# Weighted sums stored as they are and gathered by transfers, own lists at the layers' ends, all chunks between the layers normalised on ScalarE

## The chip, the core and the metric

One of the eight cores of a Trainium2 chip runs the whole program. The metric is the time of one execution in microseconds (us) on the device. The engines are TensorE (PE; its weight loads stand as PEld in the profile), VectorE (DVE), ScalarE (ACT), GpSimd (POOL) and SyncE (SP), whose queue issues all the transfers of this kernel.

## What is computed

Two transformer layers on the same activations, batch 4, sequence 1024, width 128, 16 heads of 8, all in float32. Layer 1's attention is causal; its weights are scaled up, so exact maxima matter. Both layers share the FFN weights (integers with a scale).

```python
x = x + attn_a(layernorm(x))     # qkv = x @ Wqkv + b, heads of (q 8, k 8, v 8)
x = x + ffn(layernorm(x))        # (silu(x Wg^T) * (x Wu^T)) Wd^T, hidden 384
x = x + attn_b(layernorm(x))     # as attn_a, keys after the query masked out
x = x + ffn(layernorm(x))
# attention: softmax(q k^T / sqrt(8)) v, heads side by side, @ Wout + bout
```

## The kernel before

The activations x stay in SBUF, in 8 chunks of 512 rows (4 tiles of 128). For the attention, q and k are split in two parts (for exact products in a faster format), stored to DRAM and loaded again head by head. A **window** is one batch element and a group of four heads: 16 windows per layer, of 1024 queries by 1024 keys each. A window has two **halves** f of 512 queries.

For each window there are these kinds of work, and a hand-written string of letters (`order` of a `Plan`) sets their order on every engine. The same walk over the string is run by all five engines, and each takes from it what is its own.

- `j`, a job: TensorE multiplies 128 queries by up to 512 keys (line 1146) into one bank of a ring of four (layer 1: three), and VectorE reduces it to row maxima (lines 923, masked 919, paired 900). The next job in that bank waits for it (`ring_free`). Jobs run ahead of the window to which they belong, 48 in layer 0 and 37 in layer 1.
- `h`, `H`: the negated maxima of half 0 (of the next window) or half 1, split in two bfloat16 parts by GpSimd (lines 559, 561), are turned on TensorE (line 1198), copied by ScalarE (line 696) and put by SP as two rows into the query operand (line 439), so that the score product subtracts them itself. After `H`, SP also loads the operands of the window two further on: 14 transfers.
- `s`, scores: keys by 512 queries (line 1180, causal mask 1188) for one head (layer 1: two heads), and ScalarE's exponential of it (line 680). A unit takes a bank, or a pair of banks, of the ring of units. In the last window of layer 0, from step `wide_step` = 5 on, units have two heads each (wide) in a ring of two bank pairs.
- `p`, sums: four heads' probabilities by v and a column of ones (line 1214) into bank 7. So bank 7 holds, for each head, 8 rows of sums and one of denominators, over 512 queries. After the last step of a half ScalarE copies the bank to `sums` (line 687), and the next half's sums wait for that.
- `N`, `n`: the sums of half 0 or 1 are turned: four 128x128 transposes on TensorE (line 1072), ScalarE copies the useful columns to `att_raw` (line 701), VectorE inverts the denominators (line 954), GpSimd multiplies (line 569) into `att`, rows by queries. They also take a place in the ring of units.

A window of layer 0 has 64 jobs, 64 units and 16 sums, one of layer 1 has 36, 24 and 12.

After the attention come output projection and FFN, chunk by chunk, in `turn(m, projected, ffn_rows, ffn, residual, turned, qkv_rows)`, each argument the chunk on which that step works in turn m. For chunk m+3 ScalarE gathers the heads of four windows (`gather_heads`, line 710), TensorE turns them (`transpose_ot`), ScalarE copies them (`copy_ot`, line 717). For chunk m+2: projection (line 1230), addition to x (line 831), moments (812, 816), GpSimd's inverse deviation (530, 532), normalisation (823). Chunk m+1: turn, gate and up products (1285), SiLU (781), product (1001). Chunk m: down product (1301), addition, and in layer 0 moments again and the normalisation for layer 1, on VectorE (`normalise`, line 823) for chunks 0 to 5 and on ScalarE (`normalise_tail`, line 773) for chunks 6 and 7. Chunk m-1 (layer 0): q, k, v of layer 1 (lines 1083, 1085), their split (652, 851) and store. Chunks 0 and 1 begin already in the last window (`early_chunk`, `project_at`). The first 18 to 22 jobs of layer 1 stand in the last turns of layer 0.

## Time and profile before

| | us |
|---|---|
| median of 3 runs (lowest, highest) | 1311.12 (1311.08, 1314.08) |
| the profiled execution, as timed | 1309.93 |
| its span from first to last instruction | 1308.1 |
| steady windows of layer 0, each | 39.46 |
| steady windows of layer 1, each | 25.92 |

| from, to (us) | what runs |
|---|---|
| 0 to 66 | layer 0's q, k, v, first jobs |
| 66 to 659 | windows 0 to 14 of layer 0 |
| 659 to 704 | window 15 of layer 0, with the beginnings of chunks 0 and 1 |
| 704 to 814 | projection, FFN, q, k, v of layer 1, its first jobs |
| 814 to 1215 | windows 0 to 14 of layer 1 |
| 1215 to 1242 | window 15 of layer 1 |
| 1242 to 1308 | projection and FFN of layer 1, stores |

How to read it: the page gives busy time per engine over the whole span, which mixes stages with different limits. So the stretches (busy time of each engine between two times) and the chain of waits within a stretch are of more use. Neighbouring instructions of an engine overlap, so the busy time of a group is less than count times mean, and the distance between two starts is what one costs in a row. An instruction that doesn't wait for a semaphore may still be held because its engine works in order.

### The profile page before, as it was taken

The page shows a single profiled execution, that of the slowest core. Times are in us where ns is not written, and L with a number is a line of the kernel's source. Part 1 is how long each engine was busy: PE and PEld are TensorE (multiplying, and loading weights), DVE is VectorE, ACT ScalarE, POOL GpSimd, SP SyncE. Part 2 cuts the span into 40 slices and gives each one's busy share as a digit, 9 for nine tenths or more (in the row PEclk, how much of TensorE's full clock was granted, in tenths as well). Part 3 has the DMA queues.
Part 4 walks back from the last instruction along what each step waited for, and adds up shares of the span by engine and source line. Part 5 has one row for each costly group of instructions (what it writes and reads, how often), then busy time and mean ns, then how long its engine had stood idle before and what let it go on. Part 6 is the DMA issues. An engine that isn't in the chain of part 4 may idle for free.

```text
span 1308.1 us, 26669 instructions
## 1 busy us (share of the span) xinstructions
PE 1266.3 (97%) x9681; PEld 646.3 (49%) x9681; DVE 1158.3 (89%) x2969; ACT 1005.4 (77%) x1799; POOL 148.4 (11%) x315
## 2 busy tenths in 40 slices
PE   8899999999999999999997998999999999999898
PEld 6434343434344434334334775555555555555487
DVE  8699999999999999999943888899999999999276
ACT  8678888888888888888885554677777777787743
POOL 5630000000000000000001222200000000000111
PEclk9689999999999999999998998799999999999999
DMA  7611011111011111011000263113111211220001
GB/s 217 204 33 34 16 20 34 34 35 34 9 27 34 34 34 33 6 31 35 1 3 1 65 161 97 35 37 63 37 36 41 59 37 35 45 57 3 2 26 41
DMA packets 40059, 58.43 MB, mean 45 GB/s; under 512 B 7796, under 2 KB 19448, under 8 KB 39928
## 3 DMA queue, kind: packets, MB, share of 16 engines
q1 hardware_dynamic: 39928, 56.72, 18.5%
q8 instruction: 77, 1.26, 0.4%
q14 instruction: 54, 0.44, 0.1%
HBM read 36.77 MB, written 18.87 MB: 43 GB/s over the span
## 4 chain that ended last, share of the span: by engine, by line
PE 88%; DVE 5%; ACT 3%; issue 2%; DMA 0%; POOL 0%; SPq 0%; DVEq 0%; ACTq 0%; POOLq 0%
PE psum L1214 30%; PE psum L1146 22%; PE psum L1180 20%; PE psum L1072 3%; PE psum L1301 3%; PE psum L1285 2%; PE psum L1188 2%; ACT probs L680 2%; DVE maxima L923 1%; PE psum L1083 1%; PE psum L1230 1%; DVE hid L1001 1%; PE psum L1121 1%; PE psum L1198 1%; PE psum L1057 1%
## 5 line engine op out<-in xcount | busy, mean ns | idle before, releaser
L680 ACT ACTIVATE probs<-psum 128x512 f32<-128x512 f32 (+3 forms) x1386 | 822.1, 669 | 166.1 <-PE psum L1180 87.4
L923 DVE TENSOR_REDUCE maxima<-psum 128x1 f32<-128x512 f32 x1232 | 768.4, 681 | 25.2 <-PE psum L1146 22.6
L1180 PE MATMUL psum<-qop,kop 64*128 64x512 f32 (+3 forms) x1792 | 512.7, 421 | 9.1 <-ACT probs L680 7.5
L1146 PE MATMUL psum<-kop,qop 62*128 62x512 f32 (+2 forms) x1744 | 497.9, 424 | 2.0 <-DVE maxima L919 1.0
L1214 PE MATMUL psum<-probs,v 128*32 128x512 f32 (+3 forms) x3584 | 435.4, 561 | 0.8 <-ACT sums L687 0.8
L1180 PEld LDWEIGHTS psum<-qop,kop 64*128 64x128 f32 x1792 | 254.7, 187 | 212.8 <-ACT probs L680 187.4
L1146 PEld LDWEIGHTS psum<-kop,qop 62*128 62x128 f32 x1744 | 251.2, 187 | 206.5 <-DVE maxima L923 90.7
L919 DVE CUSTOM_DVE_ANT_0 junk<-psum,mask 128x384 bf16<-128x384 f32 (+3 forms) x512 | 222.5, 485 | 14.6 <-PE psum L1146 14.0
L1214 PEld LDWEIGHTS psum<-probs,v 128*32 128x32 f32 x3584 | 72.1, 108 | 112.5 <-issue 84.5
L1188 PE MATMUL psum<-half_ident,key_mask 64*128 64x64 bf16 x1024 | 83.0, 196 | 0.0
L559 POOL TENSOR_TENSOR shift<-negmax,zeros 128x16 bf16<-128x16 f32 x64 | 14.2, 222 | 546.2 <-DVE negmax L931 546.2
L569 POOL TENSOR_TENSOR att<-att_raw,rden 128x128 f32<-128x128 f32 x64 | 26.1, 408 | 421.6 <-DVE rden L954 421.6
L1285 PE MATMUL psum<-ffn_xt,gate_up_w 128*128 128x512 f32 x192 | 53.4, 414 | 6.1 <-DVE hid L1001 6.0
L831 DVE TENSOR_TENSOR x<-psum,x 128x512 f32<-128x512 f32 x32 | 22.1, 690 | 40.2 <-PE psum L1230 26.8
L1188 PEld LDWEIGHTS psum<-half_ident,key_mask 64*128 64x128 bf16 x1024 | 45.6, 96 | 19.2 <-issue 7.9
L1301 PE MATMUL psum<-down_w,hid 128*128 128x128 f32 x384 | 47.6, 280 | 4.7 <-DVE hid L1001 4.7
L781 ACT ACTIVATE hid<-psum 128x512 f32<-128x512 f32 x48 | 28.5, 598 | 30.5 <-PE psum L1285 30.2
L1301 PEld LDWEIGHTS psum<-down_w,hid 128*128 128x128 f32 x384 | 45.0, 194 | 7.6 <-DVE hid L1001 7.2
L647 ACT ACTIVATE qk<-psum,bqk 128x512 f32<-128x512 f32 x32 | 21.2, 683 | 31.2 <-PE psum L1083 31.1
L919 DVE DVE_READ_ACCUMULATOR2_ANT maxima<- 128x1 f32 x512 | 42.5, 83 | 0.0
L1285 PEld LDWEIGHTS psum<-ffn_xt,gate_up_w 128*128 128x128 f32 x192 | 34.2, 191 | 14.8 <-DVE hid L1001 8.5
L1072 PE MATMUL psum<-ident,sums 128*128 128x128 f32 x256 | 38.7, 283 | 2.3 <-ACT sums L687 1.6
(106 smaller groups left out, 735.6 us busy)
## 6 DMA issues: line engine op xcount, KB each, us to landing
qop<-q_parts SPq DMA_DIRECT2D x256, 64.0 KB
kop<-k_parts SPq DMA_DIRECT2D x64, 128.0 KB
kop<-k_parts SPq DMA_DIRECT2D x128, 64.0 KB
q_parts<-parts SPq DMA_DIRECT2D x24, 256.0 KB, 2.9
k_parts<-parts SPq DMA_DIRECT2D x24, 256.0 KB, 3.2
x<-in_L_attn_a_x SPq DMA_DIRECT2D x8, 256.0 KB, 4.3
q_parts<-att SPq DMA_DIRECT2D x8, 256.0 KB, 3.7
k_parts<-att SPq DMA_DIRECT2D x8, 256.0 KB, 3.8
```

Of the source, the lines that this page charges most:

```text
L569: nc.gpsimd.tensor_tensor(dst, att_raw[:, f, :, :, 0:HD], rden[:, f].rearrange("p t (h o) -> p t h o", o=1).broadcast_to([P, TPC, HG, HD]) ...
L680: nc.scalar.activation(probs[:, slot, heads[0] % 2:heads[-1] % 2 + 1, c0:], psum[:, bank:bank + len(heads), c0:], ACT.Exp, scale=SCORE_SCA ...
L781: nc.scalar.activation(hid[:, c, :], psum[:, 2 + 2 * (c % 2), :], ACT.Silu, scale=DEQUANT).then_inc(silu_ready, 1)
L919: ins = nc.vector.tensor_tensor_reduce(out=junk[:, slot, column:column + width], in0=src, in1=mask[:, CHUNK - width:], scale=1.0, scalar=L ...
L923: ins = nc.vector.tensor_reduce(dst, src, AX_X, ALU.max)
L1072: ins = nc.tensor.transpose(psum[:, bank, t * P:(t + 1) * P], src[:, t, :], ident[:])
L1146: ins = mm(psum[:, bank, column:column + width], qop[rows, buf, f, r, qb * P:(qb + 1) * P].bitcast(F32R), kop[rows, buf, r, kh * CHUNK:kh ...
L1180: ins = mm(psum[:, bank + k, c0:], kop[rows, buf, c // 2, j * P:(j + 1) * P].bitcast(F32R), qop[rows, buf, f, c // 2, c0:].bitcast(F32R), ...
L1188: ins = mm(psum[:, bank + k, at:at + TILE_ROWS], key_mask[rows, part, :], half_ident[rows], start=False, stop=part == 1)
L1214: ins = mm(psum[32 * c:32 * c + 32, 7, c0:], v[:, at:at + 32], probs[:, slot, c % 2, c0:], start=(j == 0), stop=(s == plan.half_end[f]), t ...
L1285: ins = mm(psum[:, 2 + 2 * (c % 2) + k, :], gate_up_w[:, k, c, :].bitcast(F32R), ffn_xt[:, part].bitcast(F32R), start=part == 0, stop=part ...
L1301: ins = mm(psum[:, 7, t * P:(t + 1) * P], hid[:, c, t * P:(t + 1) * P], down_w[:, c, :], start=(c == 0), stop=(c == FB - 1))
```

## The change

1. The turns of the sums (`N`, `n`), their copy, the reciprocals of a half, GpSimd's products per half, the gather of the heads and the turn of a chunk with its copy are gone. Instead SP stores each `sums` tile to DRAM (`head_sums`). Per batch element it loads the denominators (as 128 rows of 64) and the heads' rows straight into `att`, which now has the width on the partitions and queries along them, as the projection wants its operand. VectorE inverts the denominators once, SP stores them and loads them broadcast over the 8 rows of a head, and GpSimd multiplies. For batch elements 0 to 2 this happens in windows 5 to 7, 9 to 11 and 13 to 15, for the last one in the turns: load after the last sums, reciprocal at the end of turn 0, product in turn 2.
2. A `Plan` has three strings, `opening`, `order` and `closing`, in place of one with offsets. In the steady windows the order of jobs, scores, sums and shifts is as it was, without `N` and `n`. The opening of layer 0 is the old one. In the opening of layer 1, 32 jobs stand before the first scores instead of 38, and 74 before window 1, as before. The closings are new: in layer 0 wide units (`S`) begin with step 4 and have a ring of three bank pairs; chunk 0 is projected at step 11 and turned for the FFN at step 14, in bank 6. In layer 1 the sums of window 14 come before the last shift.
3. `ASIDE_CHUNK` = 0: for all chunks ScalarE does the normalisation between the layers, after the second SiLU and before the third, and GpSimd the two small steps for its bias.
4. After the last window TensorE waits for the copy of the last sums, where it waited for the copy of the turned ones.

```diff
+WIDE_RING = 3
 TAIL_CHUNK = CHUNKS - 2
+ASIDE_CHUNK = 0
...
+        for letter in opening + order * (WINDOWS - 2) + closing:
+            if letter == "j":
...
+            elif letter in "sS":
+                w, x = units_begun // len(units), units[units_begun % len(units)]
+                if letter == "S":
+                    x = x[0], (x[1][0], x[1][0] + 1)
+                    self.wide_from = min(self.wide_from, taken)
+                assert letter == "S" or taken < self.wide_from
+                units_begun += 1 + (letter == "S")
...
+            return (unit - self.wide_from) % WIDE_RING * 2
+            return unit - min(unit - self.wide_from, WIDE_RING - 1)
...
 PLANS = [Plan(causal=False, heads=HEAD_UNITS, unit_ring=3, job_ring=4, alternate=True,
-              order="sjjsjpsjjjsspsjjsjspsjjsjspsjsjsjjsjssjjsjspHssjjsjpsjjsjspjjsjsspjsjssjsjjsnjsjjsspjssjsjpjssjsjpjssjsjpsjjsjspsjjsjspsjjsjsjsjsjsNhjjsjsspssjjjsps",
-              jobs_ahead=48, sums_behind=2, project_at=(9, 11, 14), wide_step=5),
+              opening="jjjjjjjjjjjjjjjjjjjjjjjjjjjjjjjjjjjjjjjjjjhjjjjjjsjjsjsjjjsssjjsjspsjjsjspsjsjsjjsjssjjsjspHssjjsjpsjjsjspjjsjsspjsjssjsjjsjsjjsspjssjsjpjssjsjpjssjsjpsjjsjspsjjsjspsjjsjsjsjsjshjjsjsspssjjjsps",
+              order="sjjsjpsjjjsspsjjsjspsjjsjspsjsjsjjsjssjjsjspHssjjsjpsjjsjspjjsjsspjsjssjsjjsjsjjsspjssjsjpjssjsjpjssjsjpsjjsjspsjjsjspsjjsjsjsjsjshjjsjsspssjjjsps",
+              closing="ssjpsjjsjspjsjjsspjjssjspsjjssjjssjjSSpSSpHSSpSSpSSpSpSSSpSpSSpSSpSSpSSpSpp",
+              jobs_paired=48, project_at=(11, 14)),
          Plan(causal=True, heads=PAIR_UNITS, unit_ring=2, job_ring=3, alternate=True,
-              order="jsjjsjHpjssjjsspjjjssppjsjsjpjjssjpjjsjspjjsjspjjsjspjjjhnNjsjjspjjsjspjjssp",
-              jobs_ahead=37, sums_behind=1, project_at=(4, 6, 10),
+              opening="jjjjjjjjjjjjjjjjjjjjjjjjjjhjjjjjjsjjsjsjsjjpjjHsjsjspjjspjssjjpjsjsjpjsjjhjssjjpjjssjjpjsjjpjjsjsjpjjsjspjsjjsp",
+              order="jsjjsjHpjssjjsspjjjssppjsjsjpjjssjpjjsjspjjsjspjjsjspjjjhjsjjspjjsjspjjssp",
+              closing="ssspHssspsspssppsspsspsspsspsspsspsspp",
+              jobs_paired=0, project_at=(6, 10),
               tiles=("230 130 330 000+020 200+220 110+310 010+210 300+320 030 100+120",
...
+CHUNK_BANKS = 6, 4
...
+    head_sums = nc.dram_tensor("head_sums", [2 * CHUNKS, GROUPS * HG, P // HG, CHUNK], F32, kind="Internal").ap()
+    scales = nc.dram_tensor("scales", [2 * CHUNKS, H, CHUNK], F32, kind="Internal").ap()
...
-        att_raw = sb("att_raw", [P, 2, TPC, HG, VH], F32)
-        rden = sb("rden", [P, 2, TPC, HG], F32)
-        att = sb("att", [P, WINDOWS, KB, HG * HD], F32)
-        early_parts = att[:].rearrange("p w k d -> p (w k d)").rearrange("p (u i t q) -> p u i t q", u=2, i=PARTS, t=2)
-        ot = sb("ot", [P, TPC, E], F32)
-        ot_t = sb("ot_t", [P, CHUNK], F32)
+        att = sb("att", [P, CHUNKS, CHUNK], F32)
+        row_scales = sb("row_scales", [P, 2, CHUNK], F32)
+        denominators = sb("denominators", [P, 2, CHUNK // HD], F32)
...
-                          ((m + 2, 1), (m + 1, 1), (m + 1, 0), (m, 0), (m + 3, 2), (m - 1 if layer == 0 else CHUNKS, 0))))
+                          ((m + 2, 1), (m + 1, 1), (m + 1, 0), (m, 0), (m - 1 if layer == 0 else CHUNKS, 0))))
...
+                def store_sums(w, f):
+                    sp.wait_ge(sums_ready, 2 * layer * WINDOWS + 2 * w + f + 1)
+                    sp.dma_start(head_sums[layer * CHUNKS + w // GROUPS * 2 + f, w % GROUPS * HG:(w % GROUPS + 1) * HG],
+                                 sums[:, f, :]).then_inc(sums_stored[f], SEM_DMA)
+                def load_sums(b):
+                    done = layer * B + b
+                    for f in range(2):
+                        sp.wait_ge(sums_stored[f], (layer * WINDOWS + (b + 1) * GROUPS) * SEM_DMA)
+                    wait(sp, scales_stored, done * 2 * SEM_DMA)
+                    wait(sp, oproj_psum, layer * CHUNKS)
+                    for f in range(2):
+                        sp.dma_start(denominators[:, f], head_sums[2 * done + f, :, HD].rearrange("h (s q) -> h s q", s=HD)).then_inc(denominators_loaded, SEM_DMA)
+                    for f in range(2):
+                        sp.dma_start(att[:, 2 * b + f], head_sums[2 * done + f, :, 0:HD]).then_inc(heads_loaded, SEM_DMA)
+                def store_scales(b):
+                    for f in range(2):
+                        sp.dma_start(scales[2 * done + f].rearrange("h (s q) -> h s q", s=HD), denominators[:, f]).then_inc(scales_stored, SEM_DMA)
+                def load_scales(b):
+                    for f in range(2):
+                        sp.dma_start(row_scales[:, f], scales[2 * done + f].rearrange("h (o q) -> h o q", o=1).broadcast_to([H, HD, CHUNK])).then_inc(heads_loaded, SEM_DMA)
                 for kind, w, number, f in plan.walk:
+                    if kind == "sums" and f in plan.half_end:
+                        store_sums(w, plan.half_end.index(f))
...
+                        if w > GROUPS and (f, w % GROUPS) == (1, 1):
+                            load_sums(w // GROUPS - 1)
+                        if w > GROUPS and (f, w % GROUPS) == (1, 2):
+                            store_scales(w // GROUPS - 1)
+                        if w > GROUPS and (f, w % GROUPS) == (0, 3):
+                            load_scales(w // GROUPS - 1)
+                load_sums(B - 1)
+                store_scales(B - 1)
+                load_scales(B - 1)
...
+                def scale_sums(b):
+                    pool.wait_ge(heads_loaded, (layer * B + b + 1) * 4 * SEM_DMA)
+                    for f in range(2):
+                        nc.gpsimd.tensor_tensor(att[:, 2 * b + f], att[:, 2 * b + f], row_scales[:, f], ALU.mult).then_inc(att_ready, 1)
-                    if kind == "norm" and f == 0 and w < WINDOWS - 1:
-                        unscaled.append(w)
-                    elif kind == "norm":
-                        scale_sums(w, f)
+                        if w > GROUPS and (f, w % GROUPS) == (1, 3):
+                            scale_sums(w // GROUPS - 1)
...
-                        if residual >= TAIL_CHUNK:
+                        if residual >= ASIDE_CHUNK:
                             negative_centre(residual, moments[:, residual % 2])
+                    if m == 2:
+                        scale_sums(B - 1)
...
+                    wait(act, sums_stored[f], (layer * WINDOWS + w) * SEM_DMA)
-                    else:
-
-                        act.wait_ge(att_ready, half_base + 2 * w + f + 1)
-                        src = psum[:, bank, :].rearrange("p (t h m) -> p t h m", t=TPC, h=HG)[:, :, :, 0:VH]
-                        nc.scalar.copy(att_raw[:, f], src).then_inc(probs_ready, 1)
-                def gather_heads(n, buf):
-                    nc.scalar.copy(ot[:].rearrange("p t (g e) -> p t g e", g=GROUPS), src).then_inc(ot_ready, 1)
-                def copy_ot(n, bank):
-                    nc.scalar.copy(ot_t[:], psum[:, bank, :]).then_inc(ot_t_ready, 1)
...
-                    if i == plan.project_at[0] - 1:
-                        act.wait_ge(att_ready, half_base + 2 * GROUPS + 2)
-                        gather_heads(0, 0)
-                    if i == plan.project_at[0]:
-                        copy_ot(0, 4)
-                    if i == plan.project_at[2]:
-                        copy_ffn_xt(0, 4)
-                        gather_heads(1, 1)
-                        copy_ot(1, 5)
+                    if i == plan.project_at[1]:
+                        copy_ffn_xt(0, CHUNK_BANKS[layer])
...
-                    if turned is not None:
-                        if m == -1:
-                            act.wait_ge(att_ready, half_base + 2 * WINDOWS + 2)
-                        gather_heads(turned, turned % 2)
-                    if turned is not None:
-                        copy_ot(turned, 0)
-                    if residual is not None and layer == 0 and residual >= TAIL_CHUNK:
+                    if residual is not None and layer == 0 and residual >= ASIDE_CHUNK:
                         normalise_tail(residual)
...
-                def invert_denominators(w, f, unit):
-                    dve.wait_ge(probs_ready, unit + 1)
-                    nc.vector.reciprocal(rden[:, f], att_raw[:, f, :, :, HD]).then_inc(rden_ready, 1)
+                def invert_denominators(b):
+                    dve.wait_ge(denominators_loaded, (layer * B + b + 1) * 2 * SEM_DMA)
+                    nc.vector.reciprocal(denominators[:], denominators[:]).then_inc(scales_ready, 1)
+                    if kind == "shift" and w > GROUPS and (what, w % GROUPS) == (0, 2):
+                        invert_denominators(w // GROUPS - 1)
-                    if residual is not None and layer == 0 and residual < TAIL_CHUNK:
+                    if residual is not None and layer == 0 and residual < ASIDE_CHUNK:
+                    if m == 0:
+                        invert_denominators(B - 1)
...
-                    else:
-                        pe.wait_ge(sums_ready, half + 1)
-                        transpose_tiles(sums[:, f, :].rearrange("p (t q) -> p t q", t=TPC), bank).then_inc(scores_ready, 1)
+                    pe.wait_ge(shift_ready, half_base + 2 * w + f + 1)
-                def transpose_ot(n, bank):
+                def project(n):
-                    pe.wait_ge(ot_ready, g + 1)
-                    transpose_tiles(ot, bank).then_inc(ot_psum, 1)
-                    pe.wait_ge(ot_t_ready, g + 1)
+                    pe.wait_ge(att_ready, g + 1)
-                        ins = mm(psum[:, 6, t * P:(t + 1) * P], ot_t[:, t * P:(t + 1) * P], wout[:, layer, :], start=True, stop=True)
+                        ins = mm(psum[:, 6, t * P:(t + 1) * P], att[:, n, t * P:(t + 1) * P], wout[:, layer, :], start=True, stop=True)
...
-                        transpose_ot(0, 4)
+                        project(0)
                     if i == plan.project_at[1]:
-                        project(0)
-                    if i == plan.project_at[2]:
-                        transpose_ffn_xn(0, 4)
-                        transpose_ot(1, 5)
+                        transpose_ffn_xn(0, CHUNK_BANKS[layer])
...
+                pe.wait_ge(sums_ready, half_base + 2 * WINDOWS)
+                        if layer == 0 and m == -1:
+                            pe.wait_ge(ffn_low_ready, 1)
                         project(projected)
-                        pe.wait_ge(ot_t_ready, min(m + 3, CHUNKS))
                         transpose_xn(CHUNKS + qkv_rows, qkv_rows % 2, 0)
-                    if turned is not None:
-                        if qkv_rows is not None:
-                            pe.wait_ge(xt_ready[0], CHUNKS + qkv_rows + 1)
-                        transpose_ot(turned, 0)
```

## Rows read from the trace of the kernel before

**Rows 1.** The page: busy us of the engine, share of span, instructions.
```profile
PE 1266.3 (97%) x9681; PEld 646.3 (49%) x9681; DVE 1158.3 (89%) x2969; ACT 1005.4 (77%) x1799; POOL 148.4 (11%) x315
```
**Rows 2.** Busy time by stretch: length, PE, PEld, DVE, ACT, POOL, clock, DMA, GB/s.
```profile
286.03:325.49 39.46, 39.24 (x271) 15.83 (x274) 39.37 (x69) 34.77 (x71) 1.70 (x6) 1.00 0.14 29
...
658.90:704.30 45.40, 40.00 (x254) 14.08 (x254) 14.92 (x35) 36.28 (x54) 2.54 (x6) 0.96 0.01 1
...
822.90:851.60 28.70, 28.60 (x255) 15.65 (x254) 24.49 (x85) 19.57 (x28) 9.76 (x5) 0.86 0.20 39
...
1021.16:1047.08 25.92, 25.88 (x270) 14.13 (x266) 23.77 (x85) 19.84 (x31) 1.66 (x6) 1.00 0.21 43
...
1214.90:1242.40 27.50, 23.43 (x249) 10.99 (x245) 4.36 (x17) 21.84 (x34) 2.89 (x7) 1.00 0.01 2
```
**Rows 3.** Who waited for whom: us in total, times, longest.
```profile
PEld psum L1146 <- DVE maxima L923: 90.7, 160, 0.8
```
**Rows 4.** Chain of waits in a window of layer 1: start, us, what.
```profile
1026.57 1.02 PE psum L1072 x8
```
**Rows 5.** In order of time, same window: start, us, instruction, idle before and releaser.
```profile
1026.22 1.89 DVE L923 TENSOR_REDUCE maxima<-psum 128x1 f32<-128x512 f32 x3 [0.46 <-PE psum L1146]
1028.02 0.35 DVE L954 RECIPROCAL rden<-att_raw 128x16 f32<-128x16 f32 x2
...
1028.16 0.18 PEld L1146 LDWEIGHTS psum<-kop,qop 62*128 62x128 f32 x1
```
**Rows 6.** Chain of waits in a window of layer 0.
```profile
299.13 0.65 PE psum L1072 x4
```
**Rows 7.** In order of time, same window: VectorE, and TensorE's weight loads.
```profile
295.13 5.58 DVE L923 TENSOR_REDUCE maxima<-psum 128x1 f32<-128x512 f32 x9
...
300.17 0.18 PEld L1146 LDWEIGHTS psum<-kop,qop 62*128 62x128 f32 x1
```
**Rows 8.** In order of time, last window of layer 0: ScalarE, VectorE.
```profile
677.20 2.85 ACT L680 ACTIVATE probs<-psum 128x1024 f32<-128x1024 f32 x3 [0.23 <-PE psum L1180]
...
657.63 11.78 DVE L923 TENSOR_REDUCE maxima<-psum 128x1 f32<-128x512 f32 x19
```
**Rows 9.** Chain of waits behind the last sums of layer 0.
```profile
704.37 0.59 ACT sums L687
...
706.14 1.14 PE psum L1230 x8
```
**Rows 10.** In order of time: ordinary turn (754.65), turn of chunk 6 (the others).
```profile
754.65 2.10 PE L1285 MATMUL psum<-ffn_xt,gate_up_w 128*128 128x512 f32 x8
...
790.11 1.64 ACT L773 ACTIVATE xn<-x,centre,moments 128x128 f32<-128x128 f32 x4
...
787.96 2.09 PE L1285 MATMUL psum<-ffn_xt,gate_up_w 128*128 128x512 f32 x8
...
793.07 0.60 PE L1301 MATMUL psum<-down_w,hid 128*128 128x128 f32 x3
```
**Rows 11.** Chain of waits in the turns of layer 0's FFN.
```profile
756.95 1.11 DVE xn L823 x4
...
760.45 2.94 PE psum L1301 x24
```
**Rows 12.** Chain of waits at the end of layer 1.
```profile
1224.34 0.61 ACT ot_t L717
...
1233.95 1.02 PE psum L1072 x8
...
1239.41 0.66 PE psum L1072 x4
```
**Rows 13.** Chain of waits in a turn of layer 1's FFN.
```profile
1263.53 0.44 PE psum L1072 x4
```
**Rows 14.** Transfers: issues with KB and us to landing; the chain at the start.
```profile
q_parts<-parts SPq DMA_DIRECT2D x24, 256.0 KB, 2.9
...
62.49 1.95 DMA qop<-shift_rows
```

144 lines of the change are left out of this document (52 added, 92 removed).

## The prediction

> **What bounds the kernel now.** I read the page first, then the busy time of each engine by stretch, then the chain of waits inside each kind of stretch, and last, engine by engine in order of time, the instructions around the steps that the change removes. The page says that TensorE is busy for 97% of the span [rows 1]. The stretches say more. A steady window of layer 0 lasts 39.46 us and has TensorE busy for 39.24 and VectorE for 39.37; one of layer 1 lasts 25.92 with 25.88 and 23.77 [rows 2]. So two engines are full in layer 0 and nearly so in layer 1. The stretches at the layers' ends are different: from 658.9 to 704.3 VectorE is busy for 14.9 of 45.4 us and ScalarE for 36.3, from 1214.9 to 1242.4 ScalarE for 21.8 of 27.5 [rows 2]. There no engine is full, and waits between them set the time.
>
> **How the two full engines are coupled.** The reader should look here before adding up TensorE time. The jobs (products for the maxima) go through a ring of four PSUM banks in layer 0 and three in layer 1; a job's weights are loaded only when VectorE has reduced the job that had its bank. The waits list has 160 weight loads of the jobs released by a plain reduction, 90.7 us together [rows 3], and the masked reductions come on top.
>
> Layer 1, around the removed turns: the eight turns of the sums take 1.02 us of the chain [rows 4]. At the same time VectorE runs three reductions, from 1026.22 to 1026.22 + 1.89 = 1028.11, and the third job after the turns loads its weights at 1028.16, 0.05 later [rows 5]. The first of these reductions had to wait for a job that TensorE issued before the turns (0.46 us idle, released by L1146) [rows 5]. So there are two ways to 1028.16, one through the turns and one through VectorE, and the second doesn't contain them. Take the turns out, and the first two jobs come earlier, the third comes when it came. The two reciprocals (1028.02, 0.35 us together) stand behind this point and before a place where VectorE is idle again, waiting for TensorE. I therefore give the 14 steady windows of layer 1 a gain of 0.
>
> Layer 0 has the same picture. The four turns before the shift take 0.59 to 0.65 us [rows 6]. Nine reductions end at 295.13 + 5.58 = 300.71, so the eighth at 300.11, and the third job after the turns loads at 300.17 [rows 7]. The other four turns (323.8) have the third job behind them at the same distance. What is left to gain is one score product that can move ahead of the held job, some 0.08 us. The window as it is has 64 reductions of 0.60 (38.3) with about 0.2 for two negations and 0.3 for two reciprocals, 38.8, and 0.7 of small waits for TensorE; without the reciprocals VectorE's floor is 38.5. I take 0.1 a window, 14.5 windows: **-1.5 us**. The bounds are 0 and 1.0 a window (39.46 to the floor), and 0 and 1.02 in layer 1.
>
> **The end of layer 0 (658.9 to 704.3).** Before, 26 units are left from step 4 on, 22 of them wide (1024 columns) in a ring of two bank pairs. Three wide exponentials in a row take 2.85 us with a last one of 1.02, so one starts 0.915 after another [rows 8]. The new list has 24 wide ones in a ring of three pairs, and ScalarE loses two copies of raw sums, two gathers and two copies of turned chunks. The jobs still all have to be reduced first: VectorE's run ends at 657.63 + 11.78 = 669.41 [rows 8]. From there: 0.5 to the first exponential, 24 x 0.915 = 22.0, the copy of the sums, of the shift and of the FFN's operand 1.2, then the last sums as before, 1.1: 694.2 instead of 704.3. TensorE's need per step is two score units 0.7 and weighted sums 1.0, 1.7 against 1.83 on ScalarE, close enough to cost something; I take 1.1 us for that. **-9 us**, bounds -3 (the list frees only what the removed copies took) and -10.
>
> **Between sums and projection.** Now the copy of the last sums starts at 704.37 and the projection of chunk 1 at 706.14, with four turns and the copy of the raw sums in between [rows 9]. Without them it starts 0.1 after the copy's end at 704.96: -1.1. All that follows (addition, moments, normalisation, gates) hangs on it. The same steps stand at the end of layer 1: -1.1. **-2.2 us**. The transfers of the last batch don't stand here, since chunks 0 and 1 were scaled long before.
>
> **The turns of layer 0's FFN.** A turn lasts 11.1 us. From the first gate product (754.65 [rows 10]) to the next down product (760.45) are 5.80, and the chain goes through VectorE's normalisation, 1.11 [rows 11]. The turn whose chunk ScalarE already normalises (790.11, 1.64 us for four) has 787.96 to 793.07, 5.11 [rows 10], though with less TensorE work. With all of it TensorE needs 2.43 to the third gate product, then 1.04, projection 0.89 and two turns of 0.44: 5.25. I take this: 0.55 less in five turns, **-2.7 us**. GpSimd gets two more small steps a chunk and, once, two scalings of 128x512; it is idle for most of a turn. If ScalarE were late by more than 0.1, its third SiLU would set the turn.
>
> **The beginning of layer 1.** 32 jobs instead of 38 stand before the first scores, 74 before window 1 in both. VectorE does them all and is busy 24.5 of 28.7 us here [rows 2], so the shift of six jobs can win only what it idles. The granted clock is 0.86 in this stretch [rows 2]: TensorE is at 1.2 GHz for part of it. **-0.5 us**, bounds -3 and +3, as it isn't shown how the clock would follow.
>
> **The end of layer 1.** The chain holds the copy of the turned chunk 0.61, eight turns 1.02, four turns 0.66 [rows 12], and beside them two gathers and another copy and turn, 4.3 in all. The store of the sums now stands before the last shift's transfer on SP, which may cost 0.5: **-3.8 us**, bounds -2 and -5.5. In the FFN's turns of this layer four turns of a chunk take 0.44 of the chain [rows 13], but the third gate product then waits for the first gate, so 0.16 in five turns: **-0.8 us**.
>
> **The transfers.** 32 stores of 256 KB, and per batch and layer a round trip: sums out, denominators and heads in, scales out, scales in. Stores of this size land 2.9 us after issue [rows 14], so the round trip is some 12 us. Three batches of four make it over three windows. The last has it beside the FFN: out at the end of the sums, the reciprocal at the end of turn 0, needed at turn 2 by GpSimd and at turn 4 by the projection. In layer 1 that is 16 us to the reciprocal and 17 from there to the scaling, against 6 for each half: hidden. I give it 0.
>
> Sum: -1.5 - 9 - 2.2 - 2.7 - 0.5 - 3.8 - 0.8 = -20.5. The profiled execution took 1309.93 (span 1308.1), so 1289.4; the median of the runs shown is 1.2 above it. I predict **1290 us**.
>
> **A rule against the sum.** After the end of layer 0 the clock is low again: the stretch's mean is 0.96 [rows 2]. I leave these losses as they are, as TensorE stays idle during the moments. The Trainium skill (TensorE: Matmul & The Clock Gate, Terms) puts the penalty of throttled time at its half. By it a closing without idle TensorE would give back up to half of the throttled time, an estimate of 1 to 3 us more; the sum doesn't use it.
>
> **Rivals.**
> *The windows shrink too.* If the third job after the turns isn't held by VectorE alone, the turns' time comes back: 14.5 x 1.0 in layer 0 (its floor) and 14 x 1.02 in layer 1, 27 us more than above: 1263; half of it is 1276. For it speaks that the chain of waits runs through the turns in each window; against it the 0.05 us between reduction and weight load. 0.14.
> *The ends don't shrink.* If in the closings the order of scores and sums on TensorE binds, only the removed steps count, some 10 us in all: 1300. For it speaks that TensorE is busy 40.0 of 45.4 us there [rows 2], against it that much of this is at single products that wait for their bank. 0.15.
> *Slower: the shift rows come late.* On SP they now share the queue with the stores. One such transfer is on the chain at the start with 1.95 us [rows 14]; after the copy of the shift, scores follow in 3.4 to 6.5 us. If the stores (2.9 us) ran in front of them, each of 64 halves would end in a wait of 1 us or more, some 60 us; it decides from a wait of 0.33 us a half, 1.4 us beyond the margin. Against it: the stores are listed steps away from the shifts. By the Trainium skill (DMA: Bandwidth & Descriptors, Queues, rings and completion order) descriptors of one ring start in order, so a store listed just before a shift would delay it; that is so only once, at the end of layer 1. 0.04, some 1320.
> *The change doesn't do what it says,* the ends staying as long as they are while the new copies and waits eat the rest: 1309 to 1315, 0.02.
>
> **How the numbers follow.** The forecast, 1282 to 1298, has 0.65. The range takes in half the case of the shrinking windows and the ends that don't shrink: 1273 to 1301. A measurement of this kernel tells 0.3% (4 us) from no change. Faster 0.94, same 0.02, slower 0.04.
>
> **What would show it.** Steady windows of 39.3 and 25.9 us, with VectorE idle a little more in layer 1; if they are 38.5 and 24.9, the ring reading is wrong. The end of layer 0 some 36 us long with wide exponentials back to back; its chunk turns 10.6 us; the end of layer 1 some 23.5 us; the weight load of the third job after the shift still 0.05 behind a reduction. A wait of scores on a transfer of shift rows, or of GpSimd on the last heads, would speak for the slower rival.

## The result, and the profile after

| | before | after |
|---|---|---|
| median of 10 runs (lowest, highest), us | 1312.76 (1309.54, 1315.45) | 1303.16 (1299.63, 1309.03) |
| mean granted clock in the profiled execution | 0.977 | 0.975 |
| profiled execution, as timed | 1309.93 | 1299.63 |

The ratio is 0.9932, 95% interval 0.992 to 0.9945. The kernel is faster, as forecast, but it gained 9.6 us where the forecast (1290) has 21, and the time lies outside the range (1273 to 1301). The profiled execution of after is the fastest of its ten runs.

The two profiled executions can be laid side by side by one mark that both have twice a window: the start of ScalarE's copy of finished sums. Column three is the time that after gained (-) or lost (+) in the stretch. "The last down product" is the first of those of the last chunk (793.07 before, 785.26 after).

| stretch | before, us | after less before | forecast |
|---|---|---|---|
| start to copy 0 | 91.75 | 0.05 | 0 |
| copies 0 to 28, fourteen windows of layer 0 | 552.28 | +3.59 | -1.4 |
| copies 28 to 31, end of layer 0 | 60.34 | -6.87 | -9 |
| copy 31 to the projection of chunk 1 | 1.77 | -0.98 | -1.1 |
| from there to the last down product | 86.93 | -3.60 | -2.7 |
| to copy 33, beginning of layer 1 | 61.37 | +0.48 | -0.5 |
| copies 33 to 61, windows of layer 1 | 363.05 | +1.47 | 0 |
| copies 61 to 63, end of layer 1 | 24.94 | -4.03 | -3.8 |
| copy 63 to the projection of chunk 1 | 1.77 | -0.98 | -1.1 |
| the rest | 63.89 | +0.57 | -0.8 |
| sum | | -10.3 | -20.4 |

So most steps at the ends came nearly as forecast, and nearly two thirds of what is missing went in the windows, where nothing was expected to be lost: 5.0 us in layer 0 and 1.5 in layer 1, of 10.1. The page of after (first its engines, then the shares of the chain that ended last):

```profile
PE 1250.3 (96%) x9361; PEld 614.2 (47%) x9361; DVE 1152.7 (89%) x2889; ACT 985.5 (76%) x1725; POOL 146.7 (11%) x279
...
PE 62%; DVE 30%; ACT 3%; issue 3%; POOL 1%; DMA 1%; SPq 0%; DVEq 0%; POOLq 0%; ACTq 0%
```

TensorE lost 16 us of busy time against [rows 1], and VectorE now holds 30% of the chain. This needs no new wait: the two ways to the third job lay 0.05 us apart, and with the turns gone the one through the reductions ends last. Busy time by stretch, columns as in [rows 2]: two windows of layer 0 without and with the batch's reciprocal, two with a fall of the clock; two of layer 1 without and with the reciprocal:

```profile
209.95:249.32 39.37, 39.05 (x260) 15.07 (x262) 39.19 (x67) 34.51 (x69) 0.88 (x4) 1.00 0.16 42
267.98:307.85 39.87, 39.46 (x260) 15.31 (x262) 39.79 (x68) 34.53 (x69) 0.88 (x4) 1.00 0.27 57
526.02:566.92 40.90, 40.60 (x260) 15.49 (x262) 39.18 (x67) 34.52 (x70) 0.88 (x4) 0.96 0.17 40
566.92:607.81 40.89, 40.58 (x260) 15.47 (x262) 39.17 (x67) 34.51 (x70) 0.88 (x4) 0.96 0.21 49
880.24:906.15 25.91, 25.38 (x261) 13.47 (x258) 23.56 (x85) 19.43 (x30) 0.87 (x4) 1.00 0.27 64
958.00:984.40 26.40, 25.86 (x261) 13.47 (x258) 24.36 (x86) 19.50 (x29) 0.87 (x4) 1.00 0.31 83
```

The plain windows are what was forecast, 39.38 and 25.92. Two things make others longer. In the third and fourth row TensorE's busy time is 1.5 us more for the same 260 products and the clock is 0.96: for 3.4 us it was granted half its speed. TensorE in order of time where the first of them begins:

```profile
536.11 0.23 PE L1193 MATMUL psum<-ident_bf,shift 128*32 128x128 bf16 x1
...
537.83 1.93 PE L1206 MATMUL psum<-probs,v 128*32 128x512 f32 x8
...
541.27 1.06 PE L1206 MATMUL psum<-probs,v 128*32 128x512 f32 x8
```

The same eight weighted sums take 1.93 and, once the clock is back, 1.06 us. In the 15 us before the fall TensorE hadn't idled. What stands there is a stretch with many score and job products, no sums for 4.3 us, and the turn of a shift; before the change the four turns of sums stood in it. The profile of before has no half clock in a steady window.

The second thing is on VectorE, in the second and the last row:

```profile
297.94 2.48 DVE L919 TENSOR_REDUCE maxima<-psum 128x1 f32<-128x512 f32 x4
300.33 0.94 DVE L950 RECIPROCAL denominators<-denominators 128x128 f32<-128x128 f32 x1
301.19 3.01 DVE L919 TENSOR_REDUCE maxima<-psum 128x1 f32<-128x512 f32 x5
```

One reciprocal of 128x128 for a whole batch stands where small ones stood in each window: 0.86 us from start to start, in the queue between reductions for which TensorE waits. The window takes 0.47 more.

The third loss is at the end. VectorE and GpSimd in a turn of layer 1's FFN:

```profile
1259.32 2.63 DVE L819 TENSOR_SCALAR ffn_xn<-x,moments 128x128 f32<-128x128 f32 x4
...
1258.84 2.52 POOL L608 TENSOR_TENSOR att<-att,row_scales 128x512 f32<-128x512 f32 x2
```

The four pieces of the normalisation, 1.1 us elsewhere, take 2.63 while GpSimd scales the last two chunks. The first piece begins inside GpSimd's first product and ends 0.1 behind it (1260.21), the second starts at that product's end (1260.12), the third at the end of the second product (1261.36). The turn lasts 8.5 us instead of 7.1. The Trainium skill (SBUF — State Buffer, Who interferes with whom) says that VectorE in a mode that takes both ports, which a tensor_scalar within SBUF can enter, and GpSimd block each other for a whole instruction; the trace agrees.

### The profile page after: what moved, and what is told of

It is laid out like the page before. It is cut to its first block, busy times and chain, and to the rows that moved or that the text cites. A ratio compares the mean times of both kernels' runs of the same rounds, so it can differ in the third digit from the quotient of the medians.

```text
span 1297.8 us, 25896 instructions
## 1 busy us (share of the span) xinstructions
PE 1250.3 (96%) x9361; PEld 614.2 (47%) x9361; DVE 1152.7 (89%) x2889; ACT 985.5 (76%) x1725; POOL 146.7 (11%) x279
## 4 chain that ended last, share of the span: by engine, by line
PE 62%; DVE 30%; ACT 3%; issue 3%; POOL 1%; DMA 1%; SPq 0%; DVEq 0%; POOLq 0%; ACTq 0%
DVE maxima L919 28%; PE psum L1206 21%; PE psum L1144 17%; PE psum L1178 12%; PE psum L1285 3%; PE psum L1269 2%; PE psum L1186 2%; PE psum L1081 1%; ACT probs L713 1%; PE psum L1216 1%; PE psum L1119 1%; DVE hid L997 1%; PE psum L1055 1%; PE psum L1070 1%; ACT hid L783 1%
## 5 line engine op out<-in xcount | busy, mean ns | idle before, releaser
L1144 PE MATMUL psum<-kop,qop 62*128 62x512 f32 (+2 forms) x1744 | 520.4, 426 | 10.8 <-DVE maxima L919 5.8
L1178 PE MATMUL psum<-qop,kop 64*128 64x512 f32 (+3 forms) x1792 | 519.2, 423 | 10.0 <-ACT probs L713 5.2
L1144 PEld LDWEIGHTS psum<-kop,qop 62*128 62x128 f32 x1744 | 256.4, 187 | 228.7 <-DVE maxima L919 116.4
L1178 PEld LDWEIGHTS psum<-qop,kop 64*128 64x128 f32 x1792 | 251.7, 187 | 216.8 <-ACT probs L713 187.4
L1269 PEld LDWEIGHTS psum<-ffn_xt,gate_up_w 128*128 128x128 f32 x192 | 34.1, 191 | 21.3 <-DVE hid L997 15.6
L997 DVE TENSOR_TENSOR hid<-psum,hid 128x512 f32<-128x512 f32 x48 | 32.2, 688 | 9.2 <-ACT hid L783 7.2
L721 ACT COPY sums<-psum 128x512 f32<-128x512 f32 x64 | 37.7, 589 | 1.7 <-PE psum L1206 1.7
```

The source lines that it names most:

```text
L721: nc.scalar.copy(sums[:, f, :], psum[:, 7, :]).then_inc(sums_ready, 1)
L997: nc.vector.tensor_tensor(hid[:, c, :], psum[:, 3 + 2 * (c % 2), :], hid[:, c, :], ALU.mult).then_inc(hid_ready, 1)
L1144: ins = mm(psum[:, bank, column:column + width], qop[rows, buf, f, r, qb * P:(qb + 1) * P].bitcast(F32R), kop[rows, buf, r, kh * CHUNK:kh ...
L1178: ins = mm(psum[:, bank + k, c0:], kop[rows, buf, c // 2, j * P:(j + 1) * P].bitcast(F32R), qop[rows, buf, f, c // 2, c0:].bitcast(F32R), ...
L1269: ins = mm(psum[:, 2 + 2 * (c % 2) + k, :], gate_up_w[:, k, c, :].bitcast(F32R), ffn_xt[:, part].bitcast(F32R), start=part == 0, stop=part ...
```

## Experiments

On the chips of these runs the kernel before had medians of 1310.0 to 1311.2 us.

**The removed turns and the clock.** Turns that nobody reads are put back, in the bank of the shift's turn:

```python
+ if layer == 0:                      # e2_fill1: layer == 1
+     for c in (1, 2, 3, 3):
+         nc.tensor.transpose(psum[:, plan.bank(number), c * P:(c + 1) * P], ident[:], ident[:])
  nc.tensor.transpose(psum[0:..., plan.bank(number), 0:P // 2].bitcast(BF16), shift..., ident_bf[:])
```

> The kernel after, with four turns of 128x128 (a unit matrix, nobody reads the result) ahead of each turn of a shift in layer 0, 0.59 us each time, where the removed turns stood. Clock theory: TensorE's clock fell in two steady windows of layer 0 because the stretch around the shift has lost its turns; with them back no window of layer 0 shows a stretch at half clock, no window lasts 40.9 us, and the median falls by 3 us or more from 1303.2 (to 1297 to 1300), with a mean granted clock of 0.977 or more in every run. Ring theory of the forecast: the 1.18 us of added TensorE work a window cost 0.1 at most (39.46 instead of 39.38). Rival (the falls are chance and have nothing to do with the turns): windows of 40.9 us stay, and the median is 1303 or above it. Rival (TensorE sets the window): windows of 40.5 us, median up by 15 us.

Measured: 1314.96 (1312.15 to 1318.65). No fall in layer 0's windows, but they last 40.1, 0.69 more. Marks twice a window show that all of it comes at one of the two shifts (that of the half 1); the other one, beside which the removed turns had stood, takes the same 0.59 us for nothing. The ring hides TensorE work at one place and not at the other, so the ring theory (0.1 at most) is wrong for the window as a whole. Of the clock theory only the windows came true: the mean clock was to be 0.977 or more in every run and was 0.967 to 0.973; in the profiled one it fell more at the layers' ends and in two windows of layer 1, which had no turns. The median says nothing for the clock, as the cost is mixed in.

> The kernel after, with the same four turns ahead of each of the two turns of a shift in layer 1, 1.0 to 1.2 us of TensorE work a window as the removed eight turns were. Ring theory: the steady windows stay at 25.92 us, as VectorE's reductions release the third job after the place, so the sum over 14 windows changes by less than 1 us and the median stays within 1 us of the kernel after. Rival (TensorE sets the window and something else gave the time back): 26.9 to 27.1 us a window, some 15 us more.

Measured: 1304.89 (1299.02 to 1305.5), 1.7 above after's median; windows of 26.20, 0.28 more for 1.18 us. Behind the one place (9 us into the window) the products are 0.01 later, behind the other 0.3. This answers the rival of shrinking windows: it is out, but the ring doesn't cover a whole window; that step of the expectation (less than 1 us in 14 windows; it was 3.6) is wrong.

So only the one place was filled. In layer 1 that is all that the change removed; in layer 0 it is half, as the other four turns of a window had stood 34.8 us into it:

```python
+ if f == 0:
+     for c in range(8 if layer else 4):
+         nc.tensor.transpose(psum[:, plan.bank(number), (1 + c % 3) * P:(2 + c % 3) * P], ident[:], ident[:])
```

> The kernel after, with the turns (of a unit matrix, nobody reads them) only ahead of the one shift of each window beside which the removed turns stood: four in layer 0, eight in layer 1. In the two kernels with turns at both shifts this place cost nothing (0.59 us of turns, 0.01 later behind them) and the other place cost 0.7 a window in layer 0 and 0.3 in layer 1. Theory (the turns at this place kept the clock up): windows of 39.4 and 25.9 to 26.1 us, no stretch at half clock in a steady window, the runs' mean clocks 0.975 to 0.981 instead of 0.966 to 0.975, a median of 1295 to 1300 instead of 1303. Rival (the falls are chance, as before or after): clocks down to 0.967 in some runs and a median of 1303 or more.

Measured: 1305.86 (1304.36 to 1306.43), clocks 0.968 to 0.970. Busy time of a window of each layer:

```profile
528.08:567.53 39.45, 39.13 (x264) 15.38 (x266) 39.23 (x67) 34.52 (x69) 0.88 (x4) 1.00 0.18 42
885.72:911.66 25.94, 25.89 (x269) 14.15 (x266) 23.61 (x85) 19.31 (x29) 0.88 (x4) 1.00 0.27 66
```

Windows: as the theory says, without a fall, and the turns are back at a cost of 0.03 and 0.01 us a window. So removing them is worth nearly nothing (for layer 0's other four, before's 39.45 against 39.38 is the bound). Median: missed. The clock fell more at other places: in the profiled execution the start is 1.9 us later, the FFN of layer 0 takes 1.1 more, the beginning of layer 1 4.5 more (30.7 us of it at half clock, after 20.5) and its end 1.3 more than in after. That keeping the clock up in the windows shortens the whole kernel is therefore not shown by this run.

The kernel after once more:

> The kernel after, unchanged, beside the others on this chip. If the place of the falls is the stretch from which the turns were removed, falls of the clock in steady windows of this profile, if there are any, begin 11.9 us behind the copy of the sums that opens a window in layer 0 (11.6 in layer 1), and two in a row are 40.9 us apart; a window with one lasts 40.9 (27.4 in layer 1). Median 1300 to 1305, mean clocks 0.966 to 0.975, spread 9 us or so. If the falls are chance anywhere, they begin at another place of the window.

Measured: 1302.92 (1301.97 to 1310.28), clocks 0.972 down to 0.963 in the slowest; before on this chip 1310.01, so the gain is 7.1 us here. Two windows of layer 1 in its profile:

```profile
931.94:959.33 27.39, 26.85 (x261) 13.89 (x258) 23.64 (x85) 19.51 (x29) 0.88 (x4) 0.94 0.28 63
959.33:986.79 27.46, 26.92 (x261) 13.85 (x258) 24.46 (x86) 19.51 (x29) 0.88 (x4) 0.94 0.35 84
```

The falls begin at 943.8 and 971.1, 11.8 and 11.7 us behind the windows' first copies, at the place that was named beforehand; in layer 0 of the same program there was none this time. Over all profiles of this study (e3's layer 1 left out, as its windows wait for GpSimd):

| passes over a layer's steady windows | passes | with falls | falls |
|---|---|---|---|
| turns at the place: before, e1 layer 0, e2 layer 1, e5, e8, e11, e13 | 12 | 0 | 0 |
| none there: after, e1 layer 1, e2 layer 0, e3 layer 0, e4, e7, e9, e10, e12 | 15 | 8 | 15 |

If turns made no difference, all eight passes with falls would lie among the fifteen in 3 cases of 1000. 14 of the 15 falls begin 11.6 to 12.0 us behind the copy that opens the window; each costs 1.5 us (1.1 in a window that holds the reciprocal). Why seven passes without turns have no fall isn't shown. Falls follow each other in neighbouring windows (three in a row in e7): a window with one in layer 0 lasts 40.9 us, and the next fall begins 40.9 to 41 later, at the same point of the window.

**The reciprocal.** First on GpSimd, as a power of -1:

```python
- nc.vector.reciprocal(denominators[:], denominators[:]).then_inc(scales_ready, 1)       # VectorE
+ nc.gpsimd.tensor_tensor(denominators[:], denominators[:], inverse[:], ALU.pow).then_inc(scales_ready, 1)
```

> The kernel after, with the reciprocal of a batch's denominators (128x32, 0.86 us on VectorE, eight times) taken from VectorE and done on GpSimd as a power of -1, at the same places in the order. Theory: in the three windows of each layer that hold it, the extra 0.45 us (39.85 instead of 39.39, 26.38 instead of 25.92) goes, 2.7 us in all. Rival (the extra time is the batch's transfers, or the shift rows held up behind them on SP): the 0.45 us stays.

(The tile is 128x128, not 128x32.) Measured: 1375.02. In layer 0 the window without the reciprocal on VectorE is a plain one, with the same transfers in it as in after (DMA 0.27, 57 GB/s in both); so the 0.47 was the reciprocal. The window behind it is 1.4 us longer, though. The three rows are these two of layer 0 and one of layer 1:

```profile
267.64:307.05 39.41, 39.09 (x260) 15.11 (x262) 39.21 (x67) 34.52 (x70) 12.72 (x5) 1.00 0.27 57
307.05:347.86 40.81, 39.20 (x260) 15.03 (x262) 39.32 (x67) 34.52 (x70) 9.79 (x5) 1.00 0.22 55
977.59:1019.08 41.49, 29.64 (x258) 15.76 (x257) 24.02 (x84) 20.00 (x29) 21.66 (x5) 0.75 0.34 75
```

The power's own group (duration in ns, least, median and most; first and last start):

```profile
L609 POOL TENSOR_TENSOR denominators<-denominators,inverse x8: 20787/20796/20819, 295.2 to 1303.9; 128x128 f32<-128x128 f32 x8
```

The power takes GpSimd 20.8 us, and the next shift's split waits behind it: in layer 0 until 316, which costs the 1.4, in layer 1's shorter windows for so long that TensorE idles and the window's clock falls to 0.75. So the expected 2.7 us were not gained anywhere, and as a remedy it is worth nothing.

Then cut, together with the mend of the last turns below. e7 inverts only 32 of the 128 elements of a partition, the rest goes on as it is; e10 inverts all:

```python
+ piece = denominators[:, part // 4, part % 4 * 16:part % 4 * 16 + 16]    # e10; e7: four of 8
+ nc.vector.reciprocal(piece, piece).then_inc(scales_ready, 1)            # after every 2nd job; e7: every 5th
```

> The kernel after with two mends and no added turns: the scaling of the last two chunks in layer 1 held back behind VectorE's normalisation (1.3 us as measured), and the batch's reciprocal on VectorE cut into four pieces of 128x8, one after every fifth job. Theory (it is the lump of 0.86 us, not VectorE's total time, that costs 0.45 us a batch): the windows with the pieces last 39.4 to 39.5 and 25.9 to 26.0 us, some 2.3 us less in all; with both mends a run without a fall of the clock takes 3.5 us less, and the median is 1299 to 1301. Rival (any time on VectorE counts here): the windows of layer 0 stay 0.4 longer, those of layer 1 do not.

> The kernel after with the last scaling in layer 1 held back behind VectorE's normalisation and the batch's reciprocal cut into eight pieces of 128x16, one after every second job. In the earlier kernel with four pieces of 128x8 (a quarter of the elements only, the rest not inverted) the windows with pieces took no extra time. Lump theory: eight pieces add at most 0.1 us a window over 39.4 and 25.95 (0.45 in one lump), so 2.3 us less over both layers, 1.3 in the last turns, 3.6 us in all from a run with the same falls of the clock; a median of 1296 to 1301. Rival (VectorE's total time counts): the windows of layer 0 stay at 39.8.

Measured: e7 1293.02 (1290.69 to 1296.96), e10 1297.54 (1295.68 to 1297.98). e7's windows are plain ones with four short pieces in them (39.39 and 25.98 us), but this was too little work to tell the lump from VectorE's time, hence e10. Of the 4.5 us between the medians some 2 are the longer pieces; the clock (0.974 to 0.980 against 0.973 to 0.976) can be a part of the rest, which isn't settled. In e10 each piece moves what follows by 0.10 us net, 0.83 in all, nearly the VectorE time of the lump:

```profile
267.76:307.25 39.49, 39.18 (x260) 15.14 (x262) 39.40 (x72) 34.59 (x70) 0.88 (x4) 1.00 0.28 57
288.52:328.22 39.70, 39.21 (x260) 14.96 (x262) 39.63 (x75) 34.59 (x69) 0.88 (x4) 1.00 0.25 53
954.69:980.97 26.28, 25.76 (x261) 13.62 (x258) 24.46 (x93) 19.42 (x30) 0.88 (x4) 1.00 0.37 86
```

A window with all eight pieces (second and third row) lasts 39.70 and 26.28 us, so a batch now costs 0.3 (layer 0) and 0.36 (layer 1) instead of 0.47. So a quarter to a third of it was the lump and the rest is VectorE's time as such; the expected 0.1 was missed. e10's median is in its range all the same.

**Two engines in the last turns.**

```python
+ if layer == 1 and b == B - 1:
+     pool.wait_ge(xn_ready[1], layer * CHUNKS + 5)      # ahead of scale_sums
```

> The kernel after, with GpSimd's scaling of the last two chunks in layer 1's FFN (two products of 128x512, 1.28 us each) held back until VectorE has normalised the chunk of that turn. Theory: the two engines hold each other up where VectorE's tensor_scalar pieces run beside GpSimd's products (VectorE's four pieces took 2.55 us instead of 1.0 there); apart, the four pieces take about 0.25 us from start to start, the turn from 1254.7 to 1263.2 lasts 7.1 to 7.2 us instead of 8.5, and all behind it comes 1.2 to 1.3 us earlier. Rival (the turn is long because the scaled heads or the transfers come late): the turn stays at 8.3 us or more.

Measured: 1302.56 (1300.54 to 1308.2), its profile with three falls in windows. VectorE, then GpSimd:

```profile
1263.62 1.11 DVE L821 TENSOR_SCALAR ffn_xn<-x,moments 128x128 f32<-128x128 f32 x4
...
1264.87 2.51 POOL L610 TENSOR_TENSOR att<-att,row_scales 128x512 f32<-128x512 f32 x2 [1.69 <-DVE ffn_xn L821]
```

1.11 us instead of 2.63; the turn lasts 7.13 instead of 8.48, and from the projection of chunk 1 to the end are 63.15 us instead of 64.46. Theory confirmed.

**The end of layer 0.**

```python
- WIDE_RING = 3
+ WIDE_RING = 2
```

> The kernel after, with the wide scores in a ring of two bank pairs instead of three and the same written order. Forecast's reading (the third pair lets TensorE run ahead, so that the wide exponentials stand back to back): from the first wide exponential to the copy of the last sums 28.5 to 32 us instead of 26.3. Rival (the third pair brings nothing, only the removed copies do): within 0.5 us of 26.3.

Measured: 28.54 us from the first wide exponential to the copy, against 26.31 in after (a single run, 1304.13); both have a fall of the clock within 0.5 us of the first wide exponential. ScalarE, of which after has three gaps and this kernel nine:

```profile
690.77 1.02 ACT L713 ACTIVATE probs<-psum 128x1024 f32<-128x1024 f32 x1 [0.19 <-PE psum L1178]
692.20 1.02 ACT L713 ACTIVATE probs<-psum 128x1024 f32<-128x1024 f32 x1 [0.41 <-PE psum L1178]
693.72 1.02 ACT L713 ACTIVATE probs<-psum 128x1024 f32<-128x1024 f32 x1 [0.50 <-PE psum L1178]
```

The third pair of banks is worth 2.2 us.

**Filling TensorE's idle time too.** e8 (with e7's reciprocals, a quarter inverted) and e11 (with e10's) add turns of a unit matrix to the mends and to the one place; e11 has the gates and the end of layer 1 besides:

```python
+ for c in range(12): nc.tensor.transpose(...)   # ahead of the wait for the last reductions of layer 0
+ for c in range(2): nc.tensor.transpose(...)    # ahead of each of 14 jobs, beginning of layer 1
+ for k in range(16 if n == 0 else 8): ...       # e11: ahead of gate 2's wait, chunks 0 and 1
+ for c in range(6): ...                         # e11: the last two shifts of layer 1
```

> Both mends, the turns of a unit matrix at the one shift of each window (four in layer 0, eight in layer 1), twelve more while TensorE waits for the last reductions ahead of layer 0's wide scores, and two ahead of each of 14 jobs at the beginning of layer 1. Theory (the rest of the missing gain is TensorE's clock): no half clock at the wide scores (1.2 us less), 10 us of it or less at the beginning of layer 1 (13.7 and 6.8 us before; 1 to 2.6 us less), no falls in windows; median 1289 to 1295, under both kernels. Rival: the added turns stand on the path themselves and eat what the clock gives: 1296 to 1300.

> The same two mends, and turns of a unit matrix wherever the profiles showed a fall of TensorE's clock: four (layer 0) and eight (layer 1) at the one shift of each window, twelve at the wait for the last reductions of layer 0, two ahead of each of 14 jobs at the beginning of layer 1, sixteen and eight at the waits for the first two chunks' gates, six at the two last shifts of layer 1. Clock theory (what is missing behind the mends is the clock): mean clocks of 0.98 or more, a spread under 5 us, a median of 1288 to 1293. Rival: the added turns cost what they give back, 1295 or more.

Measured: e8 1293.92 (1290.76 to 1295.16), clocks 0.982 to 0.985; e11 1297.70 (1297.02 to 1299.29), clocks 0.983 and 0.984. e8 did what its theory says (no half clock at the wide scores nor at the beginning of layer 1, median in its range), but e7, the same kernel without turns, is 0.9 lower, and e10, e11 without turns, 0.2 lower: over the whole kernel the added turns cost what the clock gave back. Stretches of after and of e11: the end of layer 0 from the last negation on, the FFN, the beginning of layer 1.

```profile
674.25:701.14 26.89, 26.20 (x173) 7.82 (x173) 3.76 (x14) 23.58 (x28) 4.17 (x6) 0.94 0.03 11
701.14:785.26 84.12, 74.67 (x451) 60.07 (x451) 66.48 (x216) 47.63 (x86) 24.15 (x44) 0.98 0.41 113
785.26:847.12 61.86, 57.98 (x379) 31.83 (x378) 53.33 (x192) 29.97 (x45) 17.01 (x15) 0.83 0.24 64
```

```profile
672.96:698.76 25.80, 24.93 (x175) 7.64 (x173) 3.76 (x15) 23.46 (x28) 4.20 (x6) 1.00 0.03 12
698.76:781.25 82.49, 75.63 (x476) 61.43 (x476) 66.49 (x223) 47.66 (x86) 24.15 (x44) 1.00 0.43 115
781.25:844.47 63.22, 60.56 (x423) 34.63 (x422) 54.14 (x192) 29.98 (x44) 17.02 (x15) 0.95 0.23 63
```

The clock is up in all three. It gives back 1.1 and 1.6 us in the first two. The half clock at the wide scores is gone in all three profiles with the twelve turns (e8, e11, e13) and there in all eleven without. In the third stretch the clock rises from 0.83 to 0.95, and the stretch gets 1.4 longer. e8 has the same turns there and full clock, and e2 has no turns ahead of these jobs:

```profile
783.48:843.55 60.07, 57.36 (x423) 32.96 (x422) 54.11 (x192) 29.99 (x45) 17.04 (x15) 1.00 0.24 66
783.04:842.45 59.41, 54.89 (x395) 30.85 (x395) 53.54 (x194) 30.28 (x44) 17.04 (x15) 0.91 0.25 67
```

The first is 1.8 us shorter than after's stretch, the second 2.4. Without added turns there, the stretch lasts 58.8 and 59.4 us with 10.2 us at half clock (e1, e2), 61.4 to 62.3 with 20.5 (seven profiles, before and after among them; e3 aside), 64.0 with 23.9 (e13) and 66.4 with 30.7 (e5); with them 60.1 with none (e8) and 63.2 with 6.8 (e11). So the clock is time here, some 0.25 us or more for each us at half clock, and the added turns cost more than 1 us: a net gain in e8, a net loss in e11. The start (up to the first copy) is 1.9 us later in e11 and 3.7 in e8; it has 34.1 and 37.5 us at half clock, after 30.7. For e11 the rival is right.

The last kernel keeps the mends, the place (not in a layer's first window), the wait and the gates. Its expectation takes the beginning of layer 1 from e11 (1.4 us lost) and passes over e8 (1.8 gained):

> What paid in the runs before, without what didn't: the last scaling held back, the reciprocal in four pieces of 128x32 after every fourth job, the turns of a unit matrix at the one shift of each window but not for the first window of a layer, the twelve at the last reductions of layer 0 and the sixteen and eight at the first gates; none at the beginning of layer 1 (they had cost 1.3 us there) and none more at its end. By the stages of those runs: start as in the kernel after (1.9 us less than with all turns), layer 0 up to its first down product 4 us less than the kernel after without falls, the beginning of layer 1 at its usual length, 1.4 us less in the last turns. Sum theory: 1291 to 1296 median, and no fall in a steady window. Rival: the beginning and the end of layer 1 fall more often and eat it: 1297 to 1300.

Measured: 1298.46 (1295.93 to 1298.84). No fall in a steady window, but half clock for 23.9 us at the beginning of layer 1 and 6.8 at its end (1211.9), and the start is 1.5 us later than after's though the first window has no added turns. The sum theory missed; the rival is right. e10, e11 and e13 (ratios to before 0.9899, 0.9905, 0.9899) all beat after's 1302.9 (ratio 0.9952) and can't be told from one another; e10, the smallest edit, is the one to take.

## Why the prediction missed, and what it had right

Of the 20.4 us forecast for the profiled execution 10.1 are missing. Falls of the clock in the windows took 3.0, the batch's reciprocal 2.8, the end of layer 0 2.1, GpSimd's scaling 1.4, the beginning of layer 1 1.0, a smaller gain in layer 0's windows 0.6; the FFN of layer 0 gave 0.9 more than its term. The median lies another 3.5 us above that execution.

**Steady windows: right, and the reading is shown.** 39.38 and 25.92 us for 39.3 and 25.9. In layer 1 the third job behind the place still loads 0.05 us or so after a reduction: four reductions of 0.60 begin at 889.23, the third ends near 891.1, the load is at 891.17 (TensorE's weight load, then VectorE):

```profile
891.17 0.18 PEld L1144 LDWEIGHTS psum<-kop,qop 62*128 62x128 f32 x1 [0.30 <-DVE maxima L919]
...
889.23 2.48 DVE L919 TENSOR_REDUCE maxima<-psum 128x1 f32<-128x512 f32 x4 [0.47 <-PE psum L1144]
```

Layer 0 gained 0.07 a window, not 0.1. e5 shows the same from the other side. The reading holds for the place of the removed turns alone; at the other shift (e1, e2) the same work costs 0.7 and 0.3 us a window.

**What failed first: the clock was looked at only where it was low.** The step "I leave these losses as they are" took the granted clock of the ends and supposed that the windows, 1.00 in every row of before, would keep it. That the removed turns could be what kept it wasn't among the terms, nor among the rivals. In the profiled execution it is 3.0 us. In the slower runs the clock takes more, though without profiles of them it isn't shown where: after's runs at a clock of 0.975 take 1299.6 to 1300.5, those at 0.966 and 0.967 take 1308.0 and 1309.0, while before's lie within 0.974 to 0.978 where they were recorded (1309.5 to 1312.6). That the turns at the place go with full clock there is shown (no fall in 12 passes with them, 15 falls in 15 passes without); what about them keeps the clock up isn't. Why the runs with turns in the windows lose at the ends instead (e5, e13) isn't settled.

**Second: the new reciprocal had no price in the windows.** The text takes the small ones out of VectorE's floor, and places the batch's new one only at the end. It costs 0.47 in six windows, 2.8 us: e3 (in the window that lost it) and e7 show that it is this and not the transfers; e10 shows that most of it is VectorE's time and not the lump.

**Third: GpSimd's scaling.** "It is idle for most of a turn" is true and not enough: 1.35 us for what its work does to VectorE beside it (e4). With it layer 1's FFN is +0.57; without it (e4: 63.15 us against before's 63.89) it is -0.74, the -0.8 of the forecast.

**The end of layer 0: the mechanism right, the size off by 2.1.** From the end of the last reduction to the copy the forecast has 25.9 us (24.8 and 1.1 for TensorE). With the clock kept up it is 26.0 (e8, e11, e13), in after 27.1. Besides, the last reduction ends 1.0 later in the window than before. These two are the 2.1. The rule against the sum places the 0.96 "after the end of layer 0"; the row is that of the end itself. Of the 6.9 us gained, 2.2 are the third pair (e12); how the rest splits between the new order and the removed copies wasn't tried.

**Between sums and projection, end of layer 1: right** (-0.98 and -0.98; -4.03). **FFN of layer 0: right in the turns,** which last 10.3 to 10.6 us (-2.95 in five, forecast -2.7); of the other 0.65 some 0.5 come ahead of the first down product, where before has 6.8 us at half clock and after 3.4 (e9 and e12, with 6.8, take the same 10.96 us there as before). That part is luck.

**Beginning of layer 1:** +0.48 within its bounds of 3, with 20.5 us at half clock in both; e2, whose turns stand at the shifts of layer 1, took 2.4 less, with 10.2.

**Slower rival: no.** The shift rows came at most 1.3 us late, three times in all, and transfers cost nothing that a stretch shows. Two counts in the text are off: the program has 64 stores of 256 KB (32 are one layer's), and 64 waits of 0.33 us are 21 us, which only brings the forecast back to the time of before. Neither changes the reading.

## What to carry over

Work on a hidden way is worth next to nothing to remove (here 0.07 us a window), yet it can carry something else: with the four or eight turns at the place TensorE's clock never fell in a steady window, without them it did in 8 of 15 passes. Price every instruction that a change puts into the full engine's queue, once a batch too, and look at what stands on the engine beside it. Judge a change of a few us by stages of several profiles, as a single fall of the clock is 1.5 us, and weigh a repair by the whole kernel: in e5 the windows were repaired and the clock fell more elsewhere.

## Not expected of the hardware

TensorE's clock fell to half for 3.4 us in windows in which the engine is busy for 39.05 of 39.37 us without the fall; before, with turns among the products, it didn't. With twelve turns in the wait ahead of the wide scores the clock was full behind it in three profiles of three (e8, e11, e13); without them it fell there in eleven of eleven. A power on GpSimd took 20.8 us for 128x128 elements, where VectorE's reciprocal takes 0.94.
